# Head products behind the next tile's scores, and the pairs' fold through VectorE and memory

## Chip, cores, metric

One core of a Trainium2 chip. The metric is the device time of one execution of the kernel in microseconds (us), the median of several runs.

## What is computed

The input is `x` of 4 x 1024 x 1024 floats: 4096 tokens, 32 tiles of 128 tokens with 1024 values each. Three steps follow each other, each with a layer norm in front and a residual behind:

```
x = x + 0.5 * ffn(layernorm(x))
x = x + attention(layernorm(x))
x = x + 0.5 * ffn(layernorm(x))
```

`ffn(y)` is `y @ W.T + bias`, kept only where a token and an output row are switched on. The switch comes from a softmax of `10 * y @ centroids.T` over 64 clusters: a token is on if any of its clusters is above 0.01, a row is on if its cluster is above 0.01 for any token. `attention(y)` works inside each token: q (its four heads of a group summed, as the kernel folds them), k and v are 8 groups of 32; scores are a 32 x 32 matrix per token (products of q and k over the heads, divided by sqrt(32)), softmax over its last dimension, and the product with v gives the output heads.

## The kernel before

Each 32-bit product of full precision is made of three products of split operands: `product` (L280) runs, for each of 8 blocks of 128 inputs, high x high, high x low and low x high (L285 to L287). A tile's split operand comes about in one way everywhere: ScalarE writes the normed tile, TensorE turns it in 8 transposes into `ps_t` (L292), ScalarE copies it as the high part, VectorE subtracts for the low part.

The kernel has three stages: the first feed-forward (with loading and splitting W), an attention stage, and a late stage that does what is left of the second feed-forward. This case is about the **attention stage**: a loop over i = 0 to 34, written out once per engine (TensorE L1412, ScalarE L889, VectorE L1113, GpSimd L698, SyncE's DMA queue L521). Order on an engine is the program's order; between engines there are only counting semaphores. In iteration i TensorE does, in this order:

- half of a product of the second feed-forward for an early tile (`product_third`, `ps_a`, L1358), from i = 5;
- the scores of tile i-2 (32x32 tiles, L1433), which need `k_mask` and `q_head`;
- the q and k projection of tile i-1 (512 columns, `ps_b`), the transposes of tile i-4's third norm (`transpose_third`), the v projection of tile i-1 (256 columns);
- if i is odd, from 5 to 33: the cluster logits of a pair of tiles (`pair_logits`, L295, 16 products into 256 columns of PSUM). They need the low part of tile i-4, made by `low_third` (L1108) on VectorE in the same iteration;
- the transposes of tile i's second norm (`transpose_second`, out of `y_tok`), then the head products of tile i-2 (`v_diag` times `probs`, L1479);
- if i is odd: the fold of the pair. The logits come out as clusters x tokens and in two partial sums; ScalarE has copied them to `pair_sums` (`copy_pair`, L763), and two transposes (`fold_logits`, L306) bring them to tokens x clusters in PSUM.

VectorE in iteration i: the low part of tile i-1 (`y_lo`, L1116); if i is even from 6, `pair_soft_in` (L332: copy one partial sum, add the other, maximum, subtract); `add_heads` (L1104, the attention's residual, with statistics for the third norm) of tile i-4; statistics of tile i; if i is odd from 7, `pair_soft_out` (L352, six small operations); then the softmax of the scores of tile i-2: row maximum (L1136), subtraction (L1141), turning v (L1147), row sum, reciprocal; the read of the q and k projection (`qk_read`, L1159); turning `probs` (L1162); `low_third` (L1111); the read of v (L1171).

ScalarE in iteration i: the high part of tile i-1 (L892); the copy of the head products of tile i-3 to `o_head` and their store (L899, L901); `k_mask` (four operations, L908), which waits for `k_head`; the pair's exponential; the store of the feed-forward half (L849, L853); the third norm of tile i-4 (L872); the exponential of the scores (L922); placing the values (four copies, L885); the high part of tile i-4 (L876); the norm of tile i (`y_tok`, L327).

SyncE's queue in iteration i (L521): load `f_tmp`; load v's rows; store tile i-4; load the heads of tile i-3 (`o_in`, L538, waits for their store); load a tile of x (`load_x`, L516, waits for the third norm of tile i-4); wait for `qk_read` and store q and k (L547); wait for that store and load `k_head` (L551) and `q_head` (L554); store v (L559).

Of the kernel before, what the change touches and what calls it, by code (L numbers as in the profile page):

```python
# [5 lines left out]
F32 = mybir.dt.float32  # L6
# [7 lines left out]
P = 128  # L14
# [20 lines left out]
def macaron_kernel(nc, x_in, Wq, bq, Wk, bk, Wv, bv, W, ffn_bias, centroids, assignments, out):  # L35
# [10 lines left out]
    y_d = nc.dram_tensor("y_scratch", (NT, P, EMB), F32, kind="Internal").ap()  # L46
    o_d = nc.dram_tensor("o_scratch", (NT, HKV, P, D), F32, kind="Internal").ap()


# [9 lines left out]
    with ExitStack() as ctx:  # L59
# [130 lines left out]
        def logit_at(u):  # L190
            return ps_q[:, 0, 0:QUARTER] if NP <= u < 2 * NP - 1 else ps_q[:, 3, QUARTER:HALF]

# [46 lines left out]

        late_in = w_in[0:6]  # L240
        y_last_stored = cen_in
        yl, tl, hil, lol = sem("yl"), sem("tl"), sem("hil"), sem("lol")
# [89 lines left out]
        def pair_soft_in(dve, u):  # L332

            parts = logit_at(u).rearrange("p (t s c) -> p s t c", s=2, c=NCL)
            logits = pair_exp_in[:, :].rearrange(BY_TILE, c=NCL)
            dve.wait_ge(folded, u + 1)
            wait(dve, soft_exp, u)
            dve.tensor_copy(logits, parts[:, 0]).then_inc(soft_step, 1)
            dve.wait_ge(soft_step, 7 * u + 1)
            dve.tensor_tensor(logits, logits, parts[:, 1], ALU.add).then_inc(soft_step, 1)  # L340
# [51 lines left out]
        with nc.Block() as block:  # L392
            @block.sync
            def _(sp):
# [113 lines left out]
                def load_x(t):  # L508
# [8 lines left out]
                    else:  # L517
                        sp.dma_start(x_ring[t % RING][:, :], x2_d[2 * (t - NT) + 1]).then_inc(again_in[t - NT], 16)

                BY_TOKEN_GROUP = "g (c x j) e -> x g c (j e)"  # L520
                for i in range(0, NT + 3):  # L521
# [10 lines left out]
                    if 0 <= i - 4 < NT - 2:  # L532
                        store_x2(i - 4)
                    if 0 <= i - 3 < NT:
# [5 lines left out]
                    if i == 0:  # L540
                        store_first(NT - 3)
                    if 3 <= i < NT + 1:
                        load_x(i + 1)
                    if 0 <= i - 1 < NT:
# [195 lines left out]
            def _(act):  # L740
# [22 lines left out]
                def copy_pair(u):  # L763
                    act.wait_ge(pair_done, u + 1)
                    act.copy(pair_sums[:, :], pair_ps).then_inc(pair_copied, 1)

# [107 lines left out]
                def high_third(t):  # L874
                    act.wait_ge(t3, t + 1)
                    act.copy(third_set(t)[0], ps_t[:, :, :]).then_inc(hi3, 1)  # L876

                def place_values(t):
                    act.wait_ge(v_turned, t + 1)
# [9 lines left out]
                for i in range(0, NT + 3):  # L889
# [3 lines left out]
                    if i - 1 >= NT:  # L893
                        high_again(i - 1 - NT)
                    if 0 <= i - 3 < NT:
                        t = i - 3
                        act.wait_ge(heads, t + 1)
                        wait(act, o_stored, 16 * t)
                        act.copy(o_head[:, :], ps_heads).then_inc(o_ready, 1)  # L899
                        act.wait_ge(o_ready, t + 1)  # L900
                        act.dma_start(o_d[t].rearrange("g (t r j) d -> r (g t) (j d)", t=T4, r=R4),  # L901
                                      o_head[:, :]).then_inc(o_stored, 16)
                    if 0 <= i - 2 < NT:
# [7 lines left out]
                        last.then_inc(k_ready, 1)  # L911
                    if i >= 6 and i % 2 == 0:
                        pair_soft_exp(act, NP + (i - 6) // 2)
# [26 lines left out]
                norm_third(LAST, NT + 2)  # L940
                keep_third(3)
                high_third(LAST)
                norm_late(1)
# [30 lines left out]
            def _(dve):  # L974
# [138 lines left out]
                for i in range(0, NT + 3):  # L1113
# [138 lines left out]
            def _(pe):  # L1252
# [143 lines left out]
                def product_late(v, h):  # L1396
# [10 lines left out]
                    for n, cols in enumerate(late_parts(v, h)):  # L1407
                        if n == 1:
                            pe.wait_ge(l_read[1], NL - 1)
                        product(pe, late_bank(v + n, cols), hi, lo, w_hi, w_lo, cols).then_inc(ffnl[h], 1)  # L1410

                for i in range(0, NT + 3):  # L1412
                    if 2 <= i < 5:
# [3 lines left out]
                    if 0 <= i - 2 < NT:  # L1417
# [8 lines left out]
                        pe.wait_ge(soft_in, NP + max(0, (i - 4) // 2))  # L1426
                        scores_of = ps_scores.rearrange("p r (t j e) -> p r t j e", j=2, e=D)
                        for j in range(2):
                            for c in range(T4):
                                n = 2 * c + j  # L1430
                                for r in range(R4):
# [29 lines left out]
                    if 0 <= i - 4 < NT - 2 and i % 2 == 1:  # L1461
                        u = NP + (i - 4) // 2
                        pe.wait_ge(lo3, i - 3)
                        pe.wait_ge(scores_read, min(i - 1, NT))
                        pe.wait_ge(soft_in, u)
# [5 lines left out]
                    if 0 <= i - 2 < NT:  # L1471
                        t = i - 2
                        pe.wait_ge(probs_ready, t + 1)
                        pe.wait_ge(v_ready, t + 1)
                        pe.wait_ge(scores_read, t + 1)
                        for j in range(J8):
                            for r in range(R4):
                                at = (J8 * r + j) * D
                                last = pe.matmul(ps_heads[32 * r:32 * r + 32, j * D:(j + 1) * D], v_diag[:, at:at + D],  # L1479
                                                 probs[:, at:at + D], start=True, stop=True)  # L1480
                        last.then_inc(heads, 1)
# [7 lines left out]
                pe.wait_ge(scores_read, NT)  # L1489
                pe.wait_ge(soft_in, 2 * NP - 1)  # L1490
                pair_logits(pe, odd_hi, odd_lo).then_inc(pair_done, 1)
# [40 lines left out]
```

## Time and profile before

| | |
|---|---|
| median of 3 runs | 1199.72 us (1198.96 to 1200.38) |
| profiled execution, its own time | 1198.41 us |
| its span | 1196.6 us |
| TensorE busy | 1186.3 us, 99% of the span |
| VectorE busy | 800.2 us, 67% |
| ScalarE busy | 495.5 us, 41% |
| GpSimd busy | 442.3 us, 37% |
| granted TensorE clock | full in all 40 slices |
| DMA | 208.72 MB, mean 174 GB/s |

How to read it: "busy" is the time in which an engine has an instruction under way; TensorE's products overlap, so the time from start to start counts for its pace. A wait is named by what ended it. In timelines each row is a start, a duration, the engine, the line of the program, the operation, what it writes and from what, and in brackets the idle time before it with what released it. "PEld" is TensorE's weight load, "SPq" and "ACTq" are the instructions with which SyncE and ScalarE issue DMAs.

### The profile page before, as it was taken

How to read it: one execution, taken by the hardware profiler on the slowest of the kernel's cores; microseconds unless marked ns; L12 is line 12 of the kernel's file. 1: busy time of each engine (PE TensorE's matmuls, PEld its weight loads, DVE VectorE, ACT ScalarE, POOL GpSimd, SP SyncE). 2: the span in 40 equal slices, each digit the busy share in tenths (PEclk: the TensorE clock that was granted, in tenths of full speed). 3: DMA queues.
4: the chain of work that ended last, by engine and by line, in shares of the span. 5: the costliest groups of instructions: out<-in, count | busy, mean ns of one | idle time of the engine just before them, and what ended most of it. 6: DMA issues, size and time to landing. Idle time of an engine off the chain costs nothing.

```text
span 1196.6 us, 24925 instructions
## 1 busy us (share of the span) xinstructions
PE 1186.3 (99%) x10072; PEld 1002.5 (84%) x10072; DVE 800.2 (67%) x1272; ACT 495.5 (41%) x718; POOL 442.3 (37%) x582
## 2 busy tenths in 40 slices
PE   7999999999999999999999999999999999999998
PEld 6888888888888888888888888888888888888887
DVE  6644654465454577787777877778777774299788
ACT  5322233222221355665656556566565654212110
POOL 1344445443425553433434334343343201050332
PEclk9999999999999999999999999999999999999999
DMA  7577767776664466565665555665556465017885
GB/s 276 155 203 240 209 199 188 237 206 178 160 188 147 111 163 174 144 170 139 162 168 143 168 142 159 169 145 166 153 149 169 120 173 190 5 71 254 299 284 199
DMA packets 344977, 208.72 MB, mean 174 GB/s; under 512 B 289440, under 2 KB 308640, under 8 KB 344864
## 3 DMA queue, kind: packets, MB, share of 16 engines
q1 hardware_dynamic: 329696, 187.73, 55.9%
q10 hardware_dynamic: 15168, 19.40, 4.7%
q8 instruction: 80, 1.31, 0.5%
q14 instruction: 33, 0.27, 0.1%
HBM read 118.49 MB, written 88.60 MB: 173 GB/s over the span
## 4 chain that ended last, share of the span: by engine, by line
PE 99%; DMA 0%; DVE 0%; ACT 0%; issue 0%; SPq 0%
PE ps_q L285 10%; PE ps_q L287 10%; PE ps_q L286 10%; PE ps_b L285 9%; PE ps_a L285 9%; PE ps_b L287 9%; PE ps_b L286 9%; PE ps_a L287 9%; PE ps_a L286 8%; PE ps_t L292 6%; PE ps_q L1433 3%; PE ps_q L299 3%; PE ps_q L301 2%; PE ps_q L1479 2%; PE ps_q L306 1%; DMA w_raw<-in_L_ffn_weight 0%
## 5 line engine op out<-in xcount | busy, mean ns | idle before, releaser
L318 POOL TENSOR_TENSOR var_eps<-moments,eps 128x1 f32<-128x1 f32 x96 | 18.2, 190 | 410.6 <-DVE moments L314 410.6
L285 PE MATMUL ps_a<-w_hi,odd_hi 128*128 128x512 f32 x368 | 148.1, 403 | 0.0
L287 PE MATMUL ps_a<-w_hi,odd_lo 128*128 128x512 f32 x368 | 143.8, 391 | 0.0
L286 PE MATMUL ps_a<-w_lo,odd_hi 128*128 128x512 f32 x368 | 143.4, 390 | 0.0
L635 POOL TENSOR_SCALAR f_out<-f_out,token_on 128x1024 f32<-128x1024 f32 x30 | 85.6, 2852 | 77.3 <-DVE f_out L1009 77.0
L686 POOL TENSOR_TENSOR x_ring<-x_ring,f_tmp 128x1024 f32<-128x1024 f32 x32 | 77.1, 2408 | 89.9 <-DVE best L1154 48.3
L285 PE MATMUL ps_b<-proj_hi,y_hi 128*128 128x512 f32 x256 | 103.1, 403 | 0.0
L287 PE MATMUL ps_b<-proj_hi,y_lo 128*128 128x512 f32 x256 | 100.1, 391 | 0.0
L286 PE MATMUL ps_b<-proj_lo,y_hi 128*128 128x512 f32 x256 | 99.9, 390 | 0.0
L327 ACT ACTIVATE y_tok<-x_ring,norms 128x1024 f32<-128x1024 f32 x64 | 79.7, 1245 | 42.6 <-POOL norms L323 27.5
L737 POOL TENSOR_TENSOR late<-late,mask 128x1024 f32<-128x1024 f32 x18 | 45.5, 2538 | 135.2 <-DMA late<-x_scratch 89.4
L1116 DVE TENSOR_TENSOR y_lo<-ps_t,y_hi 128x1024 fp32r<-128x1024 f32 x32 | 39.2, 1224 | 75.9 <-ACT y_hi L892 75.9
L885 ACT COPY v_diag<-part 32x256 f32<-32x256 f32 x128 | 82.5, 645 | 2.0 <-DVE part L1147 0.9
L287 PEld LDWEIGHTS ps_a<-w_hi,odd_lo 128*128 128x128 f32 x368 | 69.0, 188 | 15.2
L285 PEld LDWEIGHTS ps_a<-w_hi,odd_hi 128*128 128x128 f32 x368 | 69.1, 188 | 13.6
L286 PEld LDWEIGHTS ps_a<-w_lo,odd_hi 128*128 128x128 f32 x368 | 69.2, 188 | 13.1
L285 PE MATMUL ps_q<-w_hi,odd_hi 128*128 128x512 f32 (+1 forms) x208 | 79.5, 382 | 0.0
L287 PE MATMUL ps_q<-w_hi,odd_lo 128*128 128x512 f32 (+1 forms) x208 | 79.3, 381 | 0.0
L286 PE MATMUL ps_q<-w_lo,odd_hi 128*128 128x512 f32 (+1 forms) x208 | 79.3, 381 | 0.0
L285 PE MATMUL ps_q<-proj_hi,y_hi 128*128 128x256 f32 x256 | 74.8, 292 | 0.0
L286 PE MATMUL ps_q<-proj_lo,y_hi 128*128 128x256 f32 x256 | 72.4, 283 | 0.0
L287 PE MATMUL ps_q<-proj_hi,y_lo 128*128 128x256 f32 x256 | 72.4, 283 | 0.0
(219 smaller groups left out, 3110.8 us busy)
## 6 DMA issues: line engine op xcount, KB each, us to landing
xa<-in_L_attn_x SPq DMA_DIRECT2D x32, 512.0 KB, 5.1
f_tmp<-f_scratch SPq DMA_DIRECT2D x32, 512.0 KB, 4.6
x_ring<-in_L_attn_x SPq DMA_DIRECT2D x32, 512.0 KB, 3.6
f_scratch<-f_out SPq DMA_DIRECT2D x30, 512.0 KB, 4.0
x_scratch<-x_ring SPq DMA_DIRECT2D x30, 512.0 KB, 3.4
y_scratch<-xa SPq DMA_DIRECT2D x28, 512.0 KB, 3.7
ya_tok<-y_scratch SPq DMA_DIRECT2D x112, 128.0 KB, 3.3
late<-x_scratch SPq DMA_DIRECT2D x22, 512.0 KB, 7.0
```

Of the source, the lines that this page charges most:

```text
L285: pe.matmul(acc, hi[:, k, :], w_h[:, k, cols], start=(k == 0), stop=False)
L286: pe.matmul(acc, hi[:, k, :], w_l[:, k, cols], start=False, stop=False)
L287: last = pe.matmul(acc, lo[:, k, :], w_h[:, k, cols], start=False, stop=(k == KB - 1))
L292: last = pe.transpose(ps_t[:, k, :], src[:, k * P:(k + 1) * P], ident[:, :])
L299: last = pe.matmul(pair_ps, cen[:, k, :], hi[:, k, :, :], start=(k == 0), stop=(k == KB - 1))
L327: return act.activation(y, x, ACT.Identity, bias=norms[of][:, t, 0:1], scale=norms[of][:, t, 1:2])
L635: pool.tensor_scalar(f_out[t % 2][:, :], f_out[t % 2][:, :], token_on[0][:, t:t + 1], None, ALU.mult).then_inc(f1_on, 1)
L686: pool.tensor_tensor(x_ring[t % RING][:, :], x_ring[t % RING][:, :], f_tmp[:, :], ALU.add).then_inc(x1, 1)
L737: pool.tensor_tensor(f[:, :], f[:, :], mask[:, :], ALU.mult).then_inc(s_masked, 1)
L885: last = act.copy(v_diag[rows, :].rearrange("p (k q g c) -> p q k g c", k=R4, g=HKV, c=T4)[:, :, :, :, c], v_cols[rows, :].rearrange("p (q ...
L1116: dve.tensor_tensor(y2_lo[:, :, :], ps_t[:, :, :], y2_hi[:, :, :].bitcast(F32), ALU.subtract).then_inc(lo2, 1)
L1433: last = pe.matmul(scores_of[32 * c:32 * c + 32, r, :, j, :], q_head[rows, n * D:(n + 1) * D], k_mask[rows, n * P:(n + 1) * P].rearrange(" ...
```

## The change

In the attention stage:

- **Head products.** Those of tile i-3 now run in iteration i, directly behind the scores of tile i-2. (The last tile's keep their place at the end.) ScalarE's copy of them (`copy_heads`) moves from the top of the iteration to behind the store of the feed-forward half. VectorE's row maximum gets a wait for that copy (`o_ready`).
- **Fold.** For 15 pairs (u = 16 to 30) the two transposes on TensorE are gone. ScalarE copies the logits in another column order; VectorE turns them in 32x32 blocks (`pair_turn`, even i from 6); SyncE stores them to memory (`store_pair`) and loads them back in four pieces that put the blocks in place (`load_pair`, in even i up to 32 behind `q_in`); `pair_soft_in` waits for the load and adds the two parts in one operation. It moves to odd i, from 7, in front of `add_heads`; `pair_soft_out` moves to even i, from 8, and the exponential to odd i.
- **SyncE's order.** `load_x` and the store of the pair come in front of `o_in`.

```diff
 VectorE
+        def by_memory(u):
+            return NP <= u < 2 * NP - 1
...
         def pair_soft_in(dve, u):
...
+            if by_memory(u):
+                parts = pair_sums[:, :].rearrange("p (s h t c) -> p s t h c", s=2, h=2, c=D)
+                dve.wait_ge(pair_in, 64 * (u - NP + 1) + 16)
+                wait(dve, soft_exp, u)
+                dve.tensor_tensor(pair_exp_in[:, :].rearrange("p (t h c) -> p t h c", h=2, c=D), parts[:, 0], parts[:, 1],
+                                  ALU.add).then_inc(soft_step, 2)
...
+        def pair_turn(dve, u):
+            dve.wait_ge(pair_copied, u + 1)
+            dve.transpose(pair_sums[:, :], pair_sums[:, :]).then_inc(pair_turned, 1)
...
                     if i >= 6 and i % 2 == 0:
-                        pair_soft_in(dve, NP + (i - 6) // 2)
+                        pair_turn(dve, NP + (i - 6) // 2)
+                    if i >= 7 and i % 2 == 1:
+                        pair_soft_in(dve, NP + (i - 7) // 2)
...
-                    if i >= 7 and i % 2 == 1:
-                        pair_soft_out(dve, 1, NP + (i - 7) // 2)
+                    if i >= 8 and i % 2 == 0:
+                        pair_soft_out(dve, 1, NP + (i - 8) // 2)
...
                         dve.wait_ge(scores, t + 1)
+                        wait(dve, o_ready, t)
                         dve.reduce_max(row_max_r, scores_v, AX.X).then_inc(soft_max, 1)
...
+                pair_soft_in(dve, 2 * NP - 2)
                 low_third(LAST)
 SyncE
+                def store_pair(u):
+                    sp.wait_ge(pair_turned, u - NP + 2)
+                    sp.dma_start(pair_d, pair_sums[:, :]).then_inc(pair_stored, 16)
+
+                def load_pair(u):
+                    sp.wait_ge(pair_stored, 16 * (u - NP + 2))
+                    for b in range(T4):
+                        sp.dma_start(pair_sums[D * b:D * b + D, :].rearrange("p (h x) -> p h x", h=T4),
+                                     pair_d.rearrange("(h q) (b x) -> b q h x", q=D, b=T4)[b]).then_inc(pair_in, 16)
...
+                    if 3 <= i < NT + 1:
+                        load_x(i + 1)
+                    if i >= 6 and i % 2 == 0:
+                        store_pair(NP + (i - 6) // 2)
+                    if i > NT and i % 2 == 0:
+                        load_pair(NP + (i - 6) // 2)
                     if 0 <= i - 3 < NT:
                         t = i - 3
                         sp.wait_ge(o_stored, 16 * (t + 1))
...
                         sp.dma_start(q_head[:, :],
                                      qkv_d[t, 0:HKV].rearrange(BY_TOKEN_GROUP, c=T4, j=2)).then_inc(q_in, 16)
+                        if i >= 6 and i % 2 == 0:
+                            load_pair(NP + (i - 6) // 2)
 ScalarE
+                    if by_memory(u):
+                        act.wait_ge(soft_in, u)
+                        act.copy(pair_sums[:, :].rearrange("p (b t c) -> p t b c", t=2, c=D),
+                                 pair_ps.rearrange("p (t b c) -> p t b c", t=2, c=D)).then_inc(pair_copied, 1)
...
+                    if i >= 7 and i % 2 == 1:
+                        pair_soft_exp(act, NP + (i - 7) // 2)
...
                         store_third(i - 5)
+                    if 0 <= i - 3 < LAST:
+                        copy_heads(i - 3)
...
 TensorE
-                        wait(pe, o_ready, t)
+                        wait(pe, o_ready, t - 1)
...
                         last.then_inc(scores, 1)
+                    if 0 <= i - 3 < LAST:
+                        head_products(i - 3)
...
-                    if 0 <= i - 4 < NT - 2 and i % 2 == 1:
-                        fold_pair(NP + (i - 4) // 2)
+                    if i - 2 == LAST:
+                        head_products(LAST)
```

`head_products(t)` holds the 32 products that stood at the end of TensorE's iteration, with their waits (`probs_ready`, `v_ready`, `scores_read`) and one for `o_ready` of the tile before.

## Rows read from the trace of the kernel before

**Rows 1.** The page's chain of work that ended last, shares by engine.
```profile
PE 99%; DMA 0%; DVE 0%; ACT 0%; issue 0%; SPq 0%
```

**Rows 2.** TensorE's timeline (start, duration, line, operation), even iteration 507.65, odd 525.29.
```profile
507.46 0.44 PE L306 MATMUL ps_q<-ident,pair_sums 128*128 128x128 f32 x2
507.65 0.48 PE L285 MATMUL ps_a<-w_hi,odd_hi 128*128 128x512 f32 x1
...
514.30 0.50 PE L285 MATMUL ps_b<-proj_hi,y_hi 128*128 128x512 f32 x1
...
519.88 1.03 PE L292 MATMUL ps_t<-ident,y_tok 128*128 128x128 f32 x8
520.67 0.36 PE L285 MATMUL ps_q<-proj_hi,y_hi 128*128 128x256 f32 x1
...
523.63 1.04 PE L292 MATMUL ps_t<-ident,y_tok 128*128 128x128 f32 x8
524.60 0.76 PE L1479 MATMUL ps_q<-probs,v_diag 128*32 128x32 f32 x64
525.29 0.50 PE L285 MATMUL ps_a<-w_hi,odd_hi 128*128 128x512 f32 x1
...
541.30 0.28 PE L299 MATMUL ps_q<-odd_hi,cen 128*128 128x256 f32 x1
```

**Rows 3.** VectorE's timeline in the even iteration from 507.65.
```profile
509.06 0.28 DVE L338 COPY pair_exp_in<-ps_q 128x128 f32<-128x128 f32 x1
509.37 0.29 DVE L340 TENSOR_TENSOR pair_exp_in<-pair_exp_in,ps_q 128x128 f32<-128x128 f32 x1
...
510.22 1.22 DVE L1104 TENSOR_TENSOR x_ring<-x_ring,o_tok 128x1024 f32<-128x1024 f32 x1
...
514.45 1.18 DVE L1136 TENSOR_REDUCE norms<-ps_q 128x32 f32<-128x1024 f32 x1
...
516.81 0.43 DVE L1147 STREAM_TRANSPOSE part<-part 128x256 f32<-128x256 f32 x1
```

**Rows 4.** VectorE's timeline in the odd iteration from 525.29.
```profile
531.11 0.23 DVE L356 TENSOR_REDUCE pair_sum<-pair_exp 128x2 f32<-128x128 f32 x1
...
532.39 1.22 DVE L1136 TENSOR_REDUCE norms<-ps_q 128x32 f32<-128x1024 f32 x1
...
537.84 0.63 DVE L1159 TENSOR_TENSOR qkv_tok<-ps_b,proj_bias 128x512 f32<-128x512 f32 x1
...
539.67 1.23 DVE L1111 TENSOR_TENSOR odd_lo<-ps_t,odd_hi 128x1024 fp32r<-128x1024 f32 x1
```

**Rows 5.** ScalarE's timeline in the even iteration from 507.65.
```profile
506.87 1.01 ACT L892 CAST y_hi<-ps_t 128x1024 fp32r<-128x1024 f32 x1 [0.50 <-PE ps_t L292]
507.78 0.38 ACT L899 COPY o_head<-ps_q 128x256 f32<-128x256 f32 x1
...
516.92 1.06 ACT L922 ACTIVATE probs<-probs 128x1024 f32<-128x1024 f32 x1 [0.94 <-DVE probs L1141]
...
520.95 1.02 ACT L876 CAST odd_hi<-ps_t 128x1024 fp32r<-128x1024 f32 x1 [0.45 <-PE ps_t L292]
522.00 1.25 ACT L327 ACTIVATE y_tok<-x_ring,norms 128x1024 f32<-128x1024 f32 x1
```

**Rows 6.** SyncE's queue in the odd iteration from 525.29: start and duration of each issue.
```profile
538.49 0.37 SPq L547 DMA_DIRECT2D qkv_scratch<-qkv_tok  x1
541.47 0.54 SPq L551 DMA_DIRECT2D k_head<-qkv_scratch  x1
542.06 0.62 SPq L554 DMA_DIRECT2D q_head<-qkv_scratch  x1
542.73 0.61 SPq L559 DMA_DIRECT2D qkv_scratch<-qkv_tok  x1
```

**Rows 7.** `k_head`'s 28 loads, issue to landing; then the page's issues of `ya_tok`.
```profile
DMA to landing us min/median/max: 2.4/2.5/3.8
...
ya_tok<-y_scratch SPq DMA_DIRECT2D x112, 128.0 KB, 3.3
```

More of the change, by code:

```diff
@@ L47, in macaron_kernel @@
     o_d = nc.dram_tensor("o_scratch", (NT, HKV, P, D), F32, kind="Internal").ap()
+    pair_d = nc.dram_tensor("pair_scratch", (P, 2 * P), F32, kind="Internal").ap()
     STREAMED = list(range(0, NT - 2, 2))
@@ L190, in logit_at @@
         def logit_at(u):
-            return ps_q[:, 0, 0:QUARTER] if NP <= u < 2 * NP - 1 else ps_q[:, 3, QUARTER:HALF]
+            return ps_q[:, 3, QUARTER:HALF]
+        def by_memory(u):
+            return NP <= u < 2 * NP - 1
         def half(h):
@@ L240, in macaron_kernel @@
         late_in = w_in[0:6]
+        pair_stored, pair_in, pair_turned = w_in[6], w_in[7], cen_hi
         y_last_stored = cen_in
@@ L332, in pair_soft_in @@
         def pair_soft_in(dve, u):
-            parts = logit_at(u).rearrange("p (t s c) -> p s t c", s=2, c=NCL)
             logits = pair_exp_in[:, :].rearrange(BY_TILE, c=NCL)
[L336 to L340, printed above, removed]
+            if by_memory(u):
[4 more added lines that the diff above has]
+                                  ALU.add).then_inc(soft_step, 2)
+            else:
+                parts = logit_at(u).rearrange("p (t s c) -> p s t c", s=2, c=NCL)
+                dve.wait_ge(folded, u + 1 - (NP - 1 if u > NP else 0))
+                wait(dve, soft_exp, u)
+                dve.tensor_copy(logits, parts[:, 0]).then_inc(soft_step, 1)
+                dve.wait_ge(soft_step, 7 * u + 1)
+                dve.tensor_tensor(logits, logits, parts[:, 1], ALU.add).then_inc(soft_step, 1)
             dve.wait_ge(soft_step, 7 * u + 2)
@@ L533, in _ @@
                         store_x2(i - 4)
+                    if i == 0:
+                        store_first(NT - 3)
+                    if 3 <= i < NT + 1:
[4 more added lines that the diff above has]
+                        load_pair(NP + (i - 6) // 2)
                     if 0 <= i - 3 < NT:
@@ L539, in _ @@
                                      o_d[t].rearrange("g k d -> k g d")).then_inc(o_in, 16)
[L540 to L543, printed above, removed]
                     if 0 <= i - 1 < NT:
@@ L764, in copy_pair @@
                     act.wait_ge(pair_done, u + 1)
-                    act.copy(pair_sums[:, :], pair_ps).then_inc(pair_copied, 1)
+                    if by_memory(u):
+                        act.wait_ge(soft_in, u)
+                        act.copy(pair_sums[:, :].rearrange("p (b t c) -> p t b c", t=2, c=D),
+                                 pair_ps.rearrange("p (t b c) -> p t b c", t=2, c=D)).then_inc(pair_copied, 1)
+                    else:
+                        wait(act, soft_in, u if u > NP else 0)
+                        act.copy(pair_sums[:, :], pair_ps).then_inc(pair_copied, 1)
                 def move_kv(k):
@@ L876, in high_third, with copy_heads @@
                     act.copy(third_set(t)[0], ps_t[:, :, :]).then_inc(hi3, 1)
+                def copy_heads(t):
+                    act.wait_ge(heads, t + 1)
+                    wait(act, o_stored, 16 * t)
+                    act.copy(o_head[:, :], ps_heads).then_inc(o_ready, 1)
+                    act.wait_ge(o_ready, t + 1)
+                    act.dma_start(o_d[t].rearrange("g (t r j) d -> r (g t) (j d)", t=T4, r=R4),
+                                  o_head[:, :]).then_inc(o_stored, 16)
                 def place_values(t):
@@ L894, in _ @@
                         high_again(i - 1 - NT)
[L895 to L902, printed above, removed]
+                    if i - 3 == LAST:
+                        copy_heads(LAST)
                     if 0 <= i - 2 < NT:
@@ L911, in _ @@
                         last.then_inc(k_ready, 1)
-                    if i >= 6 and i % 2 == 0:
-                        pair_soft_exp(act, NP + (i - 6) // 2)
+                    if i >= 7 and i % 2 == 1:
+                        pair_soft_exp(act, NP + (i - 7) // 2)
                     if i == NT + 2:
@@ L941, in _ @@
                 keep_third(3)
+                pair_soft_exp(act, 2 * NP - 2)
                 high_third(LAST)
@@ L1410, in product_late, with head_products @@
                         product(pe, late_bank(v + n, cols), hi, lo, w_hi, w_lo, cols).then_inc(ffnl[h], 1)
+                def head_products(t):
+                    pe.wait_ge(probs_ready, t + 1)
+                    pe.wait_ge(v_ready, t + 1)
+                    pe.wait_ge(scores_read, t + 1)
+                    wait(pe, o_ready, t)
+                    for j in range(J8):
+                        for r in range(R4):
+                            at = (J8 * r + j) * D
+                            last = pe.matmul(ps_heads[32 * r:32 * r + 32, j * D:(j + 1) * D], v_diag[:, at:at + D],
+                                             probs[:, at:at + D], start=True, stop=True)
+                    last.then_inc(heads, 1)
                 for i in range(0, NT + 3):
@@ L1425, in _ @@
                             pe.wait_ge(m_mask, 1)
-                        pe.wait_ge(soft_in, NP + max(0, (i - 4) // 2))
+                        pe.wait_ge(soft_in, NP)
                         scores_of = ps_scores.rearrange("p r (t j e) -> p r t j e", j=2, e=D)
@@ L1464, in _ @@
                         pe.wait_ge(scores_read, min(i - 1, NT))
-                        pe.wait_ge(soft_in, u)
+                        pe.wait_ge(soft_in, NP)
+                        pe.wait_ge(pair_copied, u)
                         pair_logits(pe, odd_hi, odd_lo).then_inc(pair_done, 1)
@@ L1470, in _ @@
                         transpose_again(i - NT)
[L1471 to L1481, printed above, removed]
-                    if 0 <= i - 4 < NT - 2 and i % 2 == 1:
-                        fold_pair(NP + (i - 4) // 2)
+                    if i - 2 == LAST:
+                        head_products(LAST)
                 product_kept(3)
@@ L1489, in _ @@
                 pe.wait_ge(scores_read, NT)
-                pe.wait_ge(soft_in, 2 * NP - 1)
+                pe.wait_ge(pair_copied, 2 * NP - 1)
                 pair_logits(pe, odd_hi, odd_lo).then_inc(pair_done, 1)
```

## The prediction

> **What bounds the kernel now.** First the chain of waits, to see who sets the end: it is TensorE for 99% of the span [rows 1]. So time can only come out of TensorE's own list of instructions, or go into a hole that the change tears into it. Then TensorE's timeline over two iterations of the attention stage [rows 2]. There the reader is to see how long each piece takes from its own start to the start of the next: an iteration with even i runs from 507.65 to 525.29, 17.64 us, without a hole. Then the timelines of VectorE and ScalarE over the same iterations [rows 3 to 5], read for how close each result comes to TensorE's need of it. The closest is `low_third`: in the odd iteration it ends at 539.67 + 1.23 = 540.90 and the logits of the pair that need it start at 541.30, 0.40 us later [rows 2, 4]. ScalarE's `y_tok` for the second transposes is as near: 522.00 + 1.25 = 523.25 against 523.63 [rows 2, 5]. Any step that pushes VectorE by more than that shows in the time. Last SyncE's queue and the time a small transfer takes [rows 6, 7], since the change puts a round trip through memory there.
>
> All times below are us after the start of the 512-column product that opens an iteration; 507.65 is zero of the even one, 525.29 of the odd one.
>
> **What TensorE loses.** Fold: two transposes, 507.46 to 507.65, 0.19 us a time, in 15 iterations: 2.85 us. Head products: between plain work, the second transposes take 524.60 - 523.63 = 0.97 us to the head products, while the same eight transposes with a plain product behind them take 520.67 - 519.88 = 0.79 [rows 2]. The difference, 0.18 us, goes away for the 31 moved tiles: 5.6 us. The 0.69 of the head products themselves (524.60 to 525.29) stays. Together 8.4 us.
> Is more to be had from scores and head products side by side? The scores hand over to the projection at 514.30, behind a gap before the weights of the product that also ends a small-tile form; no row shows scores followed by head products. I bound it: if the hand-over costs what that to the projection costs, nothing changes; if it is free, up to 0.2 us a tile more is won (6 us in all, about the 0.18 just found); if both borders are paid in full, the gain of 0.18 is lost (5.6 us). I take the first, whose row is nearest, as both forms use the array in tiles but not the same ones. The Trainium skill (TensorEngine Tiling, Key Properties) says that changing the tiling mode, not just the tile, drains TensorE. By that rule scores (32 rows) to head products (128 rows) is still a change, three changes per iteration in place of four, which is the sum above, and not the free case.
>
> **What VectorE gets.** Before, the first cast of ScalarE (506.87) came while TensorE still did head products. Now the second transposes end 1.03 - 0.79 = 0.24 after the iteration's start, the cast starts at 0.28, and VectorE is through its `y_lo` 509.06 - 506.87 = 2.19 later, at 2.47 instead of 1.41 [rows 3, 5]. In the even iteration follow `pair_turn` (a transpose like that of 128x256 at 516.81, 0.45 with its gap), residual and both statistics (514.45 - 510.22 = 4.23), and `pair_soft_out`, moved here (532.39 - 531.11 = 1.28) [rows 3, 4]: VectorE comes to the row maximum at 8.43, before at 6.80. Its new wait, `o_ready`, is over earlier: head products start at 514.30 - 507.65 = 6.65, end at about 7.4, the copy takes 0.38 [rows 5], so 7.8. Behind that wait stand the score subtraction, thus the exponential, and all of VectorE's iteration; here it costs nothing because VectorE is itself later.
> ScalarE's part behind it: exponential 2.47 after the maximum starts (514.45 to 516.92), values placed 3.58 later (520.95 less the wait of 0.45, less 516.92), then cast and norm 2.30: 8.43 + 2.47 + 3.58 + 2.30 = 16.78 [rows 3, 5]. TensorE is at its second transposes at 15.98 + 0.69 = 16.67. A stall of some 0.13 us; the odd iteration starts at 16.80 + 0.79 = 17.6.
>
> **The round trip.** `pair_turn` is early in the even iteration, so the store through SyncE, behind `load_x`, is done long before it is needed, and moving `o_in` behind `load_x` and the store costs nothing while the scaled heads are wanted only in the next iteration (the cover: most of an iteration; without it each us is one of `add_heads`). The load is what counts. SyncE issues it behind `q_in`. `qk_read` starts 5.45 after the maximum (532.39 to 537.84), at 13.88; the store is issued 0.65 later, `k_in` 2.98 after that, `q_in` 0.59, the first piece of the pair 0.67 [rows 4, 6]: 18.8. Four issues: the queue's rows here lie between 0.37 and 0.67 each; I take 0.5, so the last goes at 20.3. Landing: `k_head`, same 256-byte pieces, 2.5; `ya_tok`, also in four pieces, 3.3 [rows 7]; I take 2.5, as each piece is a quarter of `k_head`'s bytes. It lands at 22.8, which is 5.2 in the odd iteration.
> By the Trainium skill (DMA: Bandwidth & Descriptors, Anatomy of one DMA) a transfer costs about 2.0 us fixed plus its bytes; that would be 2.1 here and the estimate by it is 0.4 us less per load, some 5 us less in all. The rows' 2.5 is used.
>
> **What waits for it.** `pair_soft_in` now opens the odd iteration, in front of `add_heads`, and VectorE is there at 2.47. It stands until 5.2, and behind it stand the residual, both statistics, the row maximum, everything. 5.2 + 0.85 (the pair's three operations, 510.22 - 509.37) + 4.23 = 10.3 for the maximum (7.8 if only `o_ready` held it); `low_third` starts 539.67 - 532.39 = 7.28 later and takes 1.23: 18.8 [rows 3, 4]. TensorE is at the pair's logits at 16.01 + 0.69 = 16.7. It stalls 2.0 to 2.1 us; I take 2.0. Nothing else on TensorE's list is there to fill it. The rest of the extra SyncE work (the value store behind the four issues, 2 us later) is covered: VectorE turns the values 2.4 us after the maximum starts (514.45 to 516.81), and the maximum is itself 2.5 us or more later than before.
>
> **Sum.** The stall comes in odd i from 7 to 31, 13 times; at i = 33 TensorE has a kept product before the logits and no stall. 13 x (2.0 + 0.13) = 27.7 against 8.4: +19.3. The profiled execution took 1198.4, so 1217.7; the median of the runs shown is 1.3 higher, 1219. The tail gets one more round trip, in front of the last `o_in`; the kept products cover it, as I read it, at zero, and up to 2 us if not.
> Range of this case: issues at 0.37 and a landing of 2.4 take 0.5 off each stall (6 us), free hand-overs another 6: 1207. Issues at 0.67 and a landing of 3.3 put 1.3 on each (17 us), lost hand-overs 5.6: 1241.
>
> **Rivals.** (a) Faster: the round trip is in time. The place is the wait at the head of the odd iteration; it decides at 5.2 - 2.0 = 3.2 us after the start: a pair that lands before costs nothing. Then 8.4 is kept: 1191. For it: the loads are small, VectorE is idle for a third of the span, and the store lies half an iteration ahead. Against: the queue's rows put the first issue itself at 1.2 of the odd iteration. 14%. (b) No change: the stall is a third of my size (0.7 us), so that it just eats the 8.4; it would take issues and landing 1.3 us shorter than the rows. 8%. (c) The stall is larger: four small loads behind `k_in` and `q_in` and before a 512 KB load meet a full set of DMA engines, and the late value store becomes late as well: 3.3 us each, 1236. 13%. (d) The change doesn't do what it says: head products would cost TensorE a new wait on `probs_ready`. Excluded as I read it: the probabilities are done in the iteration before. It would end like (c).
> My own case has 65%. The range goes from 1199, which takes in most of (b) and leaves out (a), to 1236, beyond which lie only the upper corner of my own case and part of (c); left out are about 2 in 10. The chance for faster by over 0.2% (2.4 us, about what a measurement can tell from no change) is 0.14, for within 0.2% 0.08, for slower 0.78.
>
> **What would show it.** In the profile of the changed kernel: a wait of VectorE at the pair's addition on the DMA into `pair_sums`, 2 to 3 us, some 13 to 15 times; idle time of TensorE before L299 of the odd iterations, released by VectorE's `odd_lo`, near 2 us each, 25 us or so in all, where there was none; even iterations near 17.6 and odd ones near 21.4. Right on the gain: transposes to the next product 0.79, no fold. I am wrong if the chain of waits is still TensorE at 99%, if the pair's wait is under 1 us, or if the hole lies before another product.

## The result, and the profile after

| | before | changed |
|---|---|---|
| median | 1199.39 us (1198.96 to 1200.38, 4 runs) | 1219.67 us (1218.65 to 1220.71, 4 runs) |
| ratio | | 1.0166, 95% interval 1.015 to 1.0181 |
| profiled execution, its own time | 1198.41 us | 1220.64 us |
| its span | 1196.6 us | 1218.8 us |

The change makes the kernel 1.7% slower. First the page of the changed kernel: the engines, and the chain of work that ended last by engine.

```profile
span 1218.8 us, 25032 instructions
...
PE 1186.9 (97%) x10042; PEld 1003.5 (82%) x10042; DVE 798.4 (66%) x1272; ACT 498.6 (41%) x718; POOL 439.1 (36%) x582
...
PE 53%; DVE 25%; DMA 8%; issue 4%; ACT 4%; SPq 4%; POOL 1%; POOLq 0%; DVEq 0%
```

TensorE has 30 instructions fewer, the fold's. It was the whole chain before [rows 1]; now it is half of it, and the rest is a loop through VectorE, ScalarE and SyncE's DMAs. The waits of TensorE and VectorE from 384 to 1020 us (total, times, longest) say where the loop closes:

```profile
PE ps_q L304 <- DVE odd_lo L1154: 19.6, 13, 2.4
```

```profile
DVE pair_exp_in L344 <- DMA pair_sums<-pair_scratch: 31.1, 14, 3.1
```

L304 is the first of the pair's logits (L299 before), L1154 is `low_third` (L1111 before), L344 is the addition in `pair_soft_in`. Before, TensorE waited for nothing in this stage. Now there are thirteen holes, one for each odd iteration from i = 7 to 31. To follow one, here is the even iteration from 626.22 and the odd one from 643.88, VectorE's timeline first (start, duration, line):

```profile
633.25 0.23 DVE L372 TENSOR_REDUCE pair_sum<-pair_exp 128x2 f32<-128x128 f32 x1
...
634.53 1.22 DVE L1182 TENSOR_REDUCE norms<-ps_q 128x32 f32<-128x1024 f32 x1
...
639.97 0.63 DVE L1205 TENSOR_TENSOR qkv_tok<-ps_b,proj_bias 128x512 f32<-128x512 f32 x1
...
645.21 1.23 DVE L1159 TENSOR_TENSOR y_lo<-ps_t,y_hi 128x1024 fp32r<-128x1024 f32 x1 [1.68 <-ACT y_hi L938]
648.39 0.29 DVE L344 TENSOR_TENSOR pair_exp_in<-pair_sums 128x128 f32<-128x128 f32 x1 [1.96 <-DMA pair_sums<-pair_scratch]
...
653.47 1.20 DVE L1182 TENSOR_REDUCE norms<-ps_q 128x32 f32<-128x1024 f32 x1
...
660.65 1.22 DVE L1154 TENSOR_TENSOR odd_lo<-ps_t,odd_hi 128x1024 fp32r<-128x1024 f32 x1
```

SyncE's queue between them:

```profile
636.43 0.42 SPq L538 DMA_DIRECT2D pair_scratch<-pair_sums  x1
637.34 0.37 SPq L572 DMA_DIRECT2D o_tok<-o_scratch  x1
640.62 0.37 SPq L577 DMA_DIRECT2D qkv_scratch<-qkv_tok  x1
643.60 0.54 SPq L581 DMA_DIRECT2D k_head<-qkv_scratch  x1
644.20 0.62 SPq L584 DMA_DIRECT2D q_head<-qkv_scratch  x1
644.87 2.03 SPq L543 DMA_DIRECT2D pair_sums<-pair_scratch  x4
```

And TensorE in the odd iteration:

```profile
643.88 0.48 PE L290 MATMUL ps_a<-w_hi,odd_hi 128*128 128x512 f32 x1
...
649.52 1.07 PE L1492 MATMUL ps_q<-k_mask,q_head 32*32 32x128 f32 x64
650.52 0.76 PE L1467 MATMUL ps_q<-probs,v_diag 128*32 128x32 f32 x64
651.21 0.50 PE L290 MATMUL ps_b<-proj_hi,y_hi 128*128 128x512 f32 x1
...
661.93 0.38 PE L304 MATMUL ps_q<-odd_hi,cen 128*128 128x256 f32 x1 [1.23 <-DVE odd_lo L1154]
```

The reader is to see the chain: the four pieces go out from 644.87, the pair is there at 648.39, VectorE has stood for it from 646.4, and everything behind it is late until `low_third` ends at 661.87 and releases TensorE at 661.93. The store of the pair went out eight microseconds before the load; nobody waits for it. The scores still take 1.00 to the next piece and the head products 0.69. Before, it was 0.69 too [rows 2], and 1.00 from this row to the projection at 514.30:

```profile
513.30 1.07 PE L1433 MATMUL ps_q<-k_mask,q_head 32*32 32x128 f32 x64
```

The holes are not all alike. Nine are of 1.02 to 1.54 us, 1.2 in the mean. The four longest, 1.77 to 2.37 us, all follow an even iteration (i = 6, 16, 20, 30) in which SyncE's issue of `q_head` takes 1.5 to 1.9 us instead of 0.62, so that the pair's pieces go out 0.5 to 1.3 us later than in the one above. That of i = 20:

```profile
760.97 1.55 SPq L584 DMA_DIRECT2D q_head<-qkv_scratch  x1
762.57 2.03 SPq L543 DMA_DIRECT2D pair_sums<-pair_scratch  x4
```

One thing in this profile stands in no row of before. It needs three stretches: an odd iteration with a hole of 1.23 us, the even one after it, and the 16 logits products behind another hole, the one that ends at 779.48 (columns: length, busy time of TensorE, its weight load, VectorE, ScalarE and GpSimd, granted clock, DMA share, GB/s):

```profile
643.88:664.70 20.82, 19.59 (x236) 16.81 (x234) 13.79 (x21) 11.46 (x18) 7.50 (x12) 1.00 0.57 151
664.70:682.37 17.67, 17.66 (x220) 14.88 (x218) 14.51 (x25) 10.71 (x16) 7.33 (x11) 1.00 0.63 167
...
779.50:782.80 3.30, 3.30 (x16) 3.30 (x17) 0.26 (x1) 0.00 (x0) 0.81 (x2) 0.53 0.34 77
```

Behind that hole the products run at a granted clock of 0.53, near the lower level of 1.2 GHz, and the logits take 3.37 us instead of 1.87. This happens behind 2 of the 13 holes, the longest (2.35 and 2.37 us); behind the next one, of 2.24 us, the clock stays at 1.00.

### The profile page after: what moved, and what is told of

Same layout as the page of the kernel before. It is cut to its first block, busy times and chain, and to the rows that moved or that the text cites. A ratio compares the mean times of both kernels' runs of the same rounds, so it can differ in the third digit from the quotient of the medians.

```text
span 1218.8 us, 25032 instructions
## 1 busy us (share of the span) xinstructions
PE 1186.9 (97%) x10042; PEld 1003.5 (82%) x10042; DVE 798.4 (66%) x1272; ACT 498.6 (41%) x718; POOL 439.1 (36%) x582
## 4 chain that ended last, share of the span: by engine, by line
PE 53%; DVE 25%; DMA 8%; issue 4%; ACT 4%; SPq 4%; POOL 1%; POOLq 0%; DVEq 0%
PE ps_q L290 6%; PE ps_q L292 6%; PE ps_q L291 6%; PE ps_b L290 4%; PE ps_b L292 4%; PE ps_b L291 4%; PE ps_a L290 4%; PE ps_a L292 4%; PE ps_a L291 4%; DMA qkv_scratch<-qkv_tok 3%; PE ps_t L297 3%; PE ps_q L304 3%; DVE probs L1187 3%; DVE norms L1195 3%; DVE bn L315 3%
## 5 line engine op out<-in xcount | busy, mean ns | idle before, releaser
L769 POOL TENSOR_TENSOR late<-late,mask 128x1024 f32<-128x1024 f32 x18 | 42.8, 2388 | 135.7 <-DMA late<-x_scratch 92.6
```

Source lines behind the costliest of these rows:

```text
L769: pool.tensor_tensor(f[:, :], f[:, :], mask[:, :], ALU.mult).then_inc(s_masked, 1)
```

## The experiments

Eight kernels, in two groups; each is compared with runs of the kernel before on the same chip. As the first stage, untouched by all of them, lets the iteration i = 2 start anywhere from 399.3 to 404.0 us, a second measure stands beside the ratio: the time in each profile from the first product of i = 2 to that of i = 34, the loop itself. Before it is 996.26 - 399.31 = 596.95 us, in the changed kernel 1018.38 - 401.78 = 616.60.

| kernel | median | ratio (interval) | loop | holes before the logits |
|---|---|---|---|---|
| before | 1199.39 | 1 | 596.95 | none |
| changed | 1219.67 | 1.0166 (1.015 to 1.0181) | +19.65 | 13, 19.6 us |
| heads_only | 1194.6 | 0.996 (0.9947 to 0.9973) | -5.10 | none |
| fold_only | 1247.73 | 1.0405 (1.0388 to 1.0422) | +50.42 | 13, 30.5 us |
| soft_in_late | 1195.09 | 0.997 (0.996 to 0.9981) | -4.18 | none |
| load_early | 1200.52 | 1.0014 (1.0001 to 1.0027) | +4.73 | 3, 2.0 us |
| soft_out_end | 1195.41 | 0.995 (0.9934 to 0.9966) | -6.71 | 2, 0.8 us |
| values_first | 1192.19 | 0.9925 (0.9909 to 0.9941) | -8.77 | none |
| load_late | 1244.15 | 1.0359 (1.034 to 1.0378) | +41.43 | 13, 28.4 us |
| fold_store_late | 1229.73 | 1.025 (1.0226 to 1.0273) | +25.71 | 13, 22.4 us |

The last four were compared with 1201.67 us for the kernel before, the first four with 1199.71; so ratios, not medians, are to be set against each other. The last two columns are those of the one execution that was profiled. In load_early that one took 1205.86 us against a median of 1200.52, so its +4.73 is more than the ratio says (1.7 us).

**heads_only.** The kernel before with one half of the change (in SyncE's queue `load_x` comes in front of `o_in`, too):

```diff
 TensorE, behind the scores
-                        wait(pe, o_ready, t)
+                        wait(pe, o_ready, t - 1)
...
+                    if 0 <= i - 3 < LAST:
+                        head_products(i - 3)
 VectorE, before the row maximum
+                        wait(dve, o_ready, t)
 ScalarE, behind store_third
+                    if 0 <= i - 3 < LAST:
+                        copy_heads(i - 3)
```

> The kernel before with the move of the head products alone (with the copy, the wait on o_ready and load_x in front of o_in); the fold stays on TensorE, the pair's softmax where it was. Theory (the cost is the pair's round trip through memory; the move itself is free and wins 0.18 us for each of 31 tiles): 1199.4 - 5.6 = 1193.8, TensorE without holes, iterations of 17.46 and 19.55 us. Rival (the later head products and the new wait hold VectorE back, and that is what makes low_third late): holes before the pair's logits of 0.5 us or more, 1200 or above.

1194.6 us, ratio 0.996. Two iterations of it, even and odd (columns as above):

```profile
509.21:526.66 17.45, 17.45 (x220) 14.88 (x218) 14.16 (x22) 11.01 (x17) 7.27 (x11) 1.00 0.59 157
526.66:546.17 19.51, 19.51 (x237) 16.95 (x236) 14.16 (x24) 11.15 (x17) 7.33 (x11) 1.00 0.60 160
```

17.64 and 19.73 before, 17.45 and 19.51 now, with no hole. So the move is worth what the two hand-overs of [rows 2] say. VectorE stands at its new wait 17 times, 9.4 us in all, and TensorE has no hole from it. The rival that puts the blame on the head products is out.

**fold_only.** The other half: the changed kernel with these lines put back.

```diff
 TensorE
-                    if 0 <= i - 3 < LAST:
-                        head_products(i - 3)
...
-                    if i - 2 == LAST:
-                        head_products(LAST)
+                    if 0 <= i - 2 < NT:
+                        head_products(i - 2)
 ScalarE: copy_heads(i - 3) at the top of the iteration again
 VectorE
-                        wait(dve, o_ready, t)
```

> The changed kernel with the head products, their copy and the row maximum's waits put back as in the kernel before; only the fold goes through VectorE and memory. Theory (the round trip alone makes the hole): VectorE waits about 2.1 us for the pair in odd iterations, TensorE stands about 1.3 us before the pair's logits, 13 times 1.3 less 2.85 is +14: 1213, up to 1216 where single loads land late. Rival (the hole needs both parts, since the head products are what makes VectorE late): 1196 to 1199.

1247.73 us: the round trip alone makes the holes, as the theory has it, but the size is missed by 34 us. One pair's wait in VectorE's timeline, in the odd iteration from 571.42, and then TensorE's waits:

```profile
576.45 0.29 DVE L344 TENSOR_TENSOR pair_exp_in<-pair_sums 128x128 f32<-128x128 f32 x1 [3.35 <-DMA pair_sums<-pair_scratch]
```

```profile
PE ps_q L304 <- DVE odd_lo L1152: 30.5, 13, 2.8
```

Two things are behind the 34 us. The first piece goes out 0.40 us into the odd iteration shown, 0.6 earlier than in the one shown of the changed kernel, but the pair is there only at 5.0 us: the pieces take 2.3 us from issue to landing in the median, up to 3.5, against 1.8 in the changed kernel. The holes become 2.35 us in the mean where I expected 1.3, some 14 us in all. And in 12 of the 13 the clock drops behind the hole: the logits take 2.4 to 3.6 us instead of 1.87, and the transposes after them up to 1.84 instead of 0.97, some 20 us in all. So a hole costs more than its length.

**soft_in_late.** The changed kernel, all transfers as they are; only the place of VectorE's wait is changed, and with it that of the exponential that follows on ScalarE:

```diff
 VectorE
-                    if i >= 7 and i % 2 == 1:
-                        pair_soft_in(dve, NP + (i - 7) // 2)
                     if 0 <= i - 4 < NT - 1:
                         add_heads(i - 4)
                     if i < NT:
                         dve.wait_ge(x1, i + 1)
                         layer_norm_stats(dve, x_ring[i % RING], 0, i, stats2, var2, norm2)
+                    if i >= 7 and i % 2 == 1:
+                        pair_soft_in(dve, NP + (i - 7) // 2)
 ScalarE: pair_soft_exp at the end of odd iterations, before copy_pair
```

> The changed kernel with the pair's first softmax part in odd iterations behind the residual and both statistics instead of in front of them, and the pair's exponential at the end of ScalarE's iteration. The same transfers at the same places. Theory: the pair has landed at 4.5 us while VectorE comes for it at about 6.7, so no wait and no hole in the odd iterations; the hole of 0.15 us in the even ones stays: 1199.4 - 8.4 + 2.5 = 1193.5 (1191 to 1196). Rival (VectorE is late through the amount or the order of its work, not through the wait): still above 1205. Rival (the transfers cost by their traffic, k_in, q_in and v behind them): still above 1205.

1195.09 us, ratio 0.997. The same place in its trace:

```profile
605.54 0.29 DVE L344 TENSOR_TENSOR pair_exp_in<-pair_sums 128x128 f32<-128x128 f32 x1
...
607.12 1.23 DVE L1182 TENSOR_REDUCE norms<-ps_q 128x32 f32<-128x1024 f32 x1 [0.65 <-ACT o_head L919]
```

No wait at L344, and the row maximum is now held by `o_ready` alone, 8.3 us into the iteration that starts at 598.84, against 9.6 in the changed kernel. Same work, same traffic, no hole before the logits: the loss was in the place of one waiting instruction in VectorE's order. What is left is the hole of the even iterations, which are still 17.66 us, and two even ones of 18.57 and 18.58 us. In these ScalarE stands 2.3 us before its copy of the heads, and the row maximum with it. The profile names no releaser, but ScalarE's own rows show what kept it: the two issues of the feed-forward store, right in front of the copy, take 2.4 us together instead of 0.8.

```profile
624.53 2.44 ACTq L891 DMA_DIRECT2D f_scratch<-f_out  x2
627.06 0.37 ACT L919 COPY o_head<-ps_q 128x256 f32<-128x256 f32 x1 [2.29 <-issue]
```

v's load, which I blamed for these two in the expectation for values_first, was in time there.

**load_early.** The other way to be in time: the transfer earlier, the wait where it is.

```diff
 SyncE, iteration i
+                        if i >= 6 and i % 2 == 0:
+                            load_pair(NP + (i - 6) // 2)
                         sp.wait_ge(qk_read, t + 1)
...
                                      qkv_d[t, 0:HKV].rearrange(BY_TOKEN_GROUP, c=T4, j=2)).then_inc(q_in, 16)
-                        if i >= 6 and i % 2 == 0:
-                            load_pair(NP + (i - 6) // 2)
```

> The changed kernel with the pair's four loads in SyncE's queue in front of the wait for qk_read instead of behind q_in. Theory: the store of the pair has landed at about 13.2 us of the even iteration, the four issues end at about 15.2, the pair lands before the odd iteration begins, VectorE doesn't wait; q and k go out 0.9 us later, which k_mask's 1.7 us of room takes: 1193.5 (1191 to 1197). Rival (the position of the load is not what counts, the four small loads collide wherever they stand): above 1205. Rival (k_in becomes the late one): holes before the scores of odd iterations, 1198 to 1206.

1200.52 us, ratio 1.0014. Position is what counts: the wait on the pair is gone from VectorE's list. But five odd iterations got a hole before the scores, and three still have one before the logits (TensorE's waits):

```profile
PE ps_q L1492 <- ACT k_mask L948: 5.5, 5, 1.9
...
PE ps_q L304 <- DVE odd_lo L1154: 2.0, 3, 1.2
```

This is the second rival: the loads push the store of q and k and then `k_head` back. In the iteration with the longest of these holes the pair's loads are issued at 675.77 to 677.51, the store of q and k at 677.56, `k_head` at 682.14, 4.6 us after that store where the changed kernel needs 3.0. `k_mask`'s room of 1.7 us took the later issue but not the slower store. The clock drops behind this hole too: it is 0.50 over the head products, which take 1.01 us instead of 0.69.

**soft_out_end.** To test where the 0.2 us of the even iterations comes from, on top of soft_in_late:

```diff
 VectorE
-                    if i >= 8 and i % 2 == 0:
-                        pair_soft_out(dve, 1, NP + (i - 8) // 2)
...
                         dve.tensor_tensor(qkv_tok[:, 2 * HD:3 * HD], ps_v, proj_bias[:, 2 * HD:3 * HD],
                                           ALU.add).then_inc(v_read, 1)
+                    if i >= 8 and i % 2 == 0:
+                        pair_soft_out(dve, 1, NP + (i - 8) // 2)
```

> As soft_in_late, and the pair's second softmax part stands at the end of VectorE's even iteration, where VectorE idles, instead of in front of the row maximum. Theory (the 0.2 us hole of the even iterations comes from these 1.28 us): the row maximum then starts at 7.8, held by o_ready alone; even iterations go from 17.66 to 17.45, 13 of them: 2.6 us under soft_in_late, 1192.3. Rival (the hole comes from the later head products and o_ready): even iterations stay at 17.66 and the time at 1195.

Even iterations take 17.47 us, so the six small operations in front of the row maximum were the cause. The loop is 2.53 us shorter than in soft_in_late; that this is the 2.6 expected is in part luck, as soft_in_late's two long even iterations (1.8 us) are gone and three odd ones are longer by 1.9 us together. The ratio, 0.995 against 0.997, does not separate the two by itself. In two of these odd iterations, with holes of 0.35 and 0.41 us, VectorE has waited 1.3 us for v's load; a third such wait, of 3.1 us, stands at i = 32.

**values_first.** One line moved in SyncE's queue on top of that:

```diff
-                        if i >= 6 and i % 2 == 0:
-                            load_pair(NP + (i - 6) // 2)
...
                         sp.dma_start(qkv_d[t, 2 * HKV:3 * HKV].rearrange("s k e -> k s e"),
                                      qkv_tok[:, 2 * HD:3 * HD].rearrange("p (s e) -> p s e", e=D)).then_inc(v_stored, 16)
+                        if i >= 6 and i % 2 == 0:
+                            load_pair(NP + (i - 6) // 2)
```

> As soft_out_end, and the pair's four loads stand behind the store of v in SyncE's queue instead of in front of it. The pair lands 0.5 us later, at about 5 us, against 6.7 at which VectorE wants it, and v is stored 2 us earlier. Theory (soft_in_late had two holes of 0.95 us where VectorE waited for v's load): these holes go too, 1190.5 to 1192. Rival (the values' load was late through traffic): same as soft_out_end.

1192.19 us, ratio 0.9925 (0.9909 to 0.9941), the lowest of all (its interval overlaps that of soft_out_end) and faster than both kernels of this case. An even and an odd iteration, and its engines:

```profile
583.63:601.12 17.49, 17.49 (x219) 14.86 (x218) 13.56 (x20) 10.79 (x16) 7.28 (x11) 1.00 0.67 171
601.12:620.42 19.30, 19.30 (x235) 16.74 (x234) 14.93 (x27) 11.38 (x18) 7.32 (x11) 1.00 0.63 166
```

```profile
PE 1179.9 (99%) x10042; PEld 1000.9 (84%) x10042; DVE 802.5 (67%) x1272; ACT 497.8 (42%) x718; POOL 441.0 (37%) x582
```

TensorE's 8.4 us are all there: the loop is 8.77 us shorter than before, and no hole before the logits or the transposes is left. Of the 3 us by which the ratio is below that of soft_out_end, 2 us are in the loop; the expectation's two holes of 0.95 us were not v's (above), but of VectorE's three waits for v's load in soft_out_end (5.8 us) one of 1.4 us is left, with no hole behind it.

**load_late.** A dose of the suspected cost, in the changed kernel itself: the same one line moved behind the store of v, and nothing else.

> The changed kernel with the one difference that the pair's four loads stand behind the store of v in SyncE's queue, one issue (0.48 us) later. A small dose of the suspected cost. Theory (each us by which the pair lands later is one us of TensorE in 13 iterations): holes of 2.0 instead of 1.5 us, 13 x 0.48 = 6 us, and where a hole now exceeds some 2 us the clock is at half for the next 3 us, as in all holes of fold_only, which adds up to 1.4 us in each: 1226 without the clock, up to 1240 with it. Rival (the landing is set by traffic and not by the place in the queue): 1219 to 1221.

1244.15 us, ratio 1.0359: half a microsecond in each of 13 loads cost some 23 us more than the changed kernel (1.0359 - 1.0166 of 1200). TensorE's waits in its trace, and two stretches, one iteration with a hole of 2.1 us and the 16 logits products behind that hole:

```profile
PE ps_q L304 <- DVE odd_lo L1154: 28.4, 13, 2.8
```

```profile
610.63:633.79 23.16, 21.04 (x235) 18.27 (x234) 13.76 (x21) 11.37 (x18) 7.21 (x11) 0.93 0.62 152
```

```profile
629.55:633.00 3.45, 3.45 (x16) 3.45 (x17) 0.27 (x1) 0.00 (x0) 0.30 (x1) 0.53 0.38 84
```

The holes grow from 1.5 to 2.2 us in the mean, 0.7 for a dose of 0.48, which is 9 us. The rest is the clock: the logits take over 2.3 us in 10 of 13 iterations (3.2 to 3.6 in most), 1.97 in the others. The direction and the clock's part are as the theory says, but its "all holes of fold_only" was 12 of 13, and the time is 4 us beyond its upper figure (2.5 by the ratio).

**fold_store_late.** For the late landings in fold_only, the suspect was ScalarE's store of the heads, which goes out in the same moment as the pair's loads:

```diff
 ScalarE
                     act.copy(o_head[:, :], ps_heads).then_inc(o_ready, 1)
+
+                def store_heads(t):
                     act.wait_ge(o_ready, t + 1)
...
                         store_third(i - 5)
+                    if 0 <= i - 3 < LAST:
+                        store_heads(i - 3)
```

> As fold_only, and ScalarE issues the store of the heads' copy behind the store of the feed-forward half instead of right after the copy. In fold_only this store (ScalarE's queue) goes out in the same moment as the pair's loads, which land 2.3 us after their issue instead of 1.8. Theory (that store is what makes them late, the holes pass 2 us and the clock falls to half behind each): landings at 1.8 again, holes of 1.3 to 1.6 us, no clock loss in most: 1212 to 1222. Rival (the landings are late for another reason): 1240 or above.

1229.73 us lies between the two. The pieces land after 1.9 us in the median instead of 2.3, the mean hole is 1.7 instead of 2.35, and the clock drops behind 2 holes instead of 12: most of fold_only's extra is gone with that store. But eight landings still take 2.9 to 3.5 us. They come in four pairs: each time one issue takes 1.5 to 1.8 us instead of 0.44, and that piece and the one before it land late. What makes an issue that long stays open.

## Why the prediction was right

The forecast was 1219, the measurement 1219.67; the mechanism is the one forecast, shown by soft_in_late and load_early, which take it away in two ways, and by load_late, which adds to it. That the sum came within 1 us is luck, as the account at the end shows: its terms are off by more, in both directions.

- **What TensorE loses** (8.4 us): right. Head products 0.18 a tile, fold 0.19 a pair: most iterations take 17.44 and 19.30 in values_first against 17.64 and 19.73, loop -8.77. From the scores to the head products it is 1.00 us from start to start, as to the projection before: the value taken between the free case and the full one was right. The Trainium skill (TensorEngine Tiling (Array Packing), Key Properties) says that a change of tiling mode drains TensorE. The trace agrees: the step from scores to head products is no cheaper than that from scores to a plain product (649.52 to 650.52 against 513.30 to 514.30).
- **What VectorE gets**: right. The row maximum of the even iteration starts at 634.53 - 626.22 = 8.31, forecast 8.43, and the read of the q and k projection at 13.75, forecast 13.88. VectorE reaches the pair at 646.4 - 643.88 = 2.5, forecast 2.47. The even iteration's hole was forecast at 0.13 us and is 0.2 (17.67 against 17.44 to 17.47).
- **The round trip**: the landing was taken too late. First piece at 18.65, forecast 18.8; the four issues at 0.51 each, forecast 0.5; but the last piece lands after 1.7 to 1.9 us, not 2.5. The pair is there at 4.5 into the odd iteration, not 5.2, in the iteration shown. The Trainium skill (DMA: Bandwidth & Descriptors, Anatomy of one DMA) gives a fixed cost of about 2.0 us plus the bytes, fitted to DMAs that GpSimd issues. The estimate by it, 2.1, was nearer to these loads of SyncE's than the row of a transfer four times as large.
- **The hole**: forecast 2.0 to 2.1 each, measured 19.6 / 13 = 1.5, from 1.0 to 2.4. By this term the change would have been about 6.5 us cheaper. Without the four long issues of `q_head`, for which the sum had no term, it would be about 1.2.
- **The clock**: this was missing from the sum. Behind the two longest holes the logits took 1.5 to 1.6 us more than 1.87, and behind the others 0.1 more.

The loop's own account: 13 odd iterations are longer by the hole and by 0.16 us that the wait's record leaves out (in the one shown the v projection lasts 4.35 us to the logits instead of 2.96, with a hole of 1.23), which is 21.7; the even ones 12 x 0.2 = 2.4; the logits behind the holes 13 x 0.1 = 1.3, and 2.8 more behind the two at the lower clock; less 8.4: 19.8 against 19.65 measured. The forecast had 19.3: its holes were 6.4 us too large, and the even ones (0.7 too small), the 0.16 a hole (2.1) and the slower logits (4.1) make up 6.9. The first stage began the loop 2.5 us later in this profile; the kernels with the same first stage differ by as much, so this is no part of the change.
Rival (a) had the right place, and the change missed its point of decision, 3.2 us into the odd iteration, by 1.3 us. Its price, 1191, is reached only by values_first (0.9925), with three further moves; with the wait alone moved it is 0.997, with the loads alone moved 1.0014.

## What to carry to other kernels

When work goes off the busiest engine through memory, ask first where in the receiving engine's order the wait stands and what is queued behind it: here the same transfers cost 20 us with the wait in front of the residual, and the loop is 24 us shorter with the wait behind the residual and both statistics, 4.2 us of VectorE's work later. A small load behind others in one queue is late by the issues in front of it as much as by its own time, and moving it forward makes those behind it late. The safe place is the one with room on both sides, and a half-microsecond on the queue can be worth 2%. The room must also take an issue that for once lasts 1 to 2 us longer.

## What was not expected of the hardware

- The price of a hole in TensorE is not its length. Holes up to 1.77 us cost themselves and about 0.3 us more (0.16 before the logits, 0.1 in them). Of the 32 holes of 1.84 to 2.8 us before the logits in the changed kernel, fold_only, load_late and fold_store_late, 26 were followed by products at a reduced granted clock (0.53 over 3.3 us in the changed kernel, over 3.45 us in load_late). The logits then took 0.5 to 1.7 us more than 1.87, about 1.4 or more in 20 of the 26. Length alone does not decide it: holes of 1.84 and 1.87 us in load_late were followed by slower products, and others of 2.24 us in the changed kernel and 2.28 us in fold_store_late were not. Which condition decides stays open.
- A load of 32 KB in 256-byte pieces lands 1.8 us after its issue in the median in the changed kernel, and 2.3 in fold_only, where ScalarE's queue issues a 128 KB store at the same time; with that store later, in fold_store_late, it is 1.9. Single ones take up to 3.5 us in either of these two.
- The time of an issue is not fixed. In every kernel of this case, the one before included, 6 to 17 of the 380 to 460 DMA issues of SyncE and ScalarE between 384 and 1000 us take 0.6 to 2.0 us longer than the same instruction mostly does. In the kernel before, one of 2.25 us at 569.25 tears no hole into TensorE; in the changed kernel and in soft_in_late they stand on the path and set the longest holes. What makes them long stays open.
